# Last attention step: the initial state's reset-gate product and the last probabilities' transposes ahead of the other tile's transposed attention

## The reference, cut to what matters

```python
x = x + attn(cond(x, ...), W_attn, b_attn, W_proj, b_proj)       # 32 heads of 8 features, causal softmax
x = x + ffn(gru(cond_2048, x, W_ih, W_hh, b_ih, b_hh), weight, scale_weight, bias)
return x

# gru, one step; the initial h is cond_2048 (128, 256)
gi = x_t @ W_ih + b_ih          # i_r, i_z, i_n
gh = h @ W_hh + b_hh            # h_r, h_z, h_n
r = sigmoid(i_r + h_r); z = sigmoid(i_z + h_z)
n = tanh(i_n + r * h_n)
h = (1 - z) * n + z * h
```

## Time and profile before

| | us |
|---|---|
| median of 3 runs | 446.46 |
| lowest, highest | 446.11, 447.05 |
| the profiled execution, whole | 447.21 |
| its span, first to last instruction | 445.4 |
| PE busy in the span | 425.4 (95%) |
| DVE, ACT, POOL busy | 329.2, 234.5, 89.9 |

### The profile page before, as it was taken

How to read it: one execution, slowest core, us unless ns; L and a number is a source line. 1 busy time by engine, 2 the same in 40 slices (tenths; PEclk the granted TensorE clock), 3 DMA queues, 4 the chain that set the end, 5 groups by cost and what they waited for, 6 DMA issues and landing times.

```text
span 445.4 us, 13421 instructions
## 1 busy us (share of the span) xinstructions
PE 425.4 (95%) x5448; PEld 351.7 (79%) x5448; DVE 329.2 (74%) x1001; ACT 234.5 (53%) x547; POOL 89.9 (20%) x108
## 2 busy tenths in 40 slices
PE   8799899999999999999999899999999999999994
PEld 6556687786778777787787688899999999999984
DVE  3596888798788887888778945566777767777665
ACT  7254748566575576755766653444444444444341
POOL 7662233333132221322235300000000000000000
PEclk9989999999999999999999999999999999999999
DMA  8941513314132141331212100001010000000001
GB/s 293 396 173 44 154 34 90 90 50 119 31 93 91 49 119 40 91 92 55 74 29 83 38 1 1 1 2 47 1 49 18 30 24 26 24 25 25 24 25 71
DMA packets 34268, 30.36 MB, mean 68 GB/s; under 512 B 4128, under 2 KB 29344, under 8 KB 34208
## 3 DMA queue, kind: packets, MB, share of 16 engines
q1 hardware_dynamic: 34208, 29.51, 20.3%
HBM read 16.92 MB, written 8.39 MB: 57 GB/s over the span
## 4 chain that ended last, share of the span: by engine, by line
PE 75%; DVE 14%; ACT 4%; issue 3%; SPq 2%; DMA 1%; POOL 1%; DVEq 0%; ACTq 0%; POOLq 0%
PE ps_a L1243 9%; PE ps_s L1406 7%; PE ps_t L1406 6%; PE ps_o L1406 6%; PE ps_s L1303 6%; PE ps_s L1462 5%; PE ps_t L1462 5%; PE ps_a L1462 4%; PE ps_m L1462 4%; PE ps_t L1316 4%; PE ps_m L1345 4%; PE ps_o L1327 3%; PE ps_m L1337 2%; ACT y L586 2%; DVE st L889 2%
## 5 line engine op out<-in xcount | busy, mean ns | idle before, releaser
L528 POOL TENSOR_TENSOR sc<-masked,mx 128x512 f32<-128x512 f32 x32 | 45.7, 1429 | 144.1 <-DVE mx L939 144.1
L1243 PE MATMUL ps_a<-yT_r,w_qkv_r 128*128 128x512 f32 x180 | 46.0, 403 | 1.3 <-DVE yT_r L912 0.9
L931 DVE COPY_PREDICATED masked<-kst,ps_s 128x512 f32<-128x512 int32 x64 | 43.9, 734 | 2.9 <-PE ps_s L1303 2.5
L730 ACT ACTIVATE zg<-ps_t,brz 128x128 f32<-128x128 f32 x64 | 20.1, 365 | 39.7 <-PE ps_t L1406 37.4
L939 DVE TENSOR_REDUCE mx<-masked 128x16 f32<-128x512 f32 x64 | 40.5, 674 | 0.0
L624 ACT ACTIVATE sc<-sc 128x512 f32<-128x512 f32 x64 | 37.3, 622 | 5.5 <-DVE sc L945 4.2
L1243 PEld LDWEIGHTS ps_a<-yT_r,w_qkv_r 128*128 128x128 f32 x180 | 32.6, 188 | 9.6 <-issue 2.8
L1077 DVE SCALAR_TENSOR_TENSOR rg<-ps_o,vec,rg 128x128 f32<-128x128 f32 x64 | 19.5, 346 | 24.6 <-PE ps_o L1406 23.6
L557 ACT ACTIVATE pT<-ps_t 128x512 f32<-128x512 f32 x64 | 34.8, 595 | 4.9 <-PE ps_t L1316 3.6
L1406 PEld LDWEIGHTS ps_s<-hT,w_hh 128*128 128x128 f32 x256 | 33.1, 191 | 5.0 <-DVE hT L1095 2.9
L1303 PE MATMUL ps_s<-kbd,qn 64*32 64x256 f32 x1024 | 36.0, 382 | 0.0
(11 more groups left out here) (157 smaller groups left out, 828.1 us busy)
## 6 DMA issues: line engine op xcount, KB each, us to landing
xf<-in_x_feat SPq DMA_DIRECT2D x8, 512.0 KB, 9.5
xg<-in_x_tok SPq DMA_DIRECT2D x8, 512.0 KB, 4.0
kbd<-kn SPq DMA_DIRECT2D x128, 32.0 KB, 1.9
v_dram<-vn SPq DMA_DIRECT2D x16, 256.0 KB, 3.3
vbd<-v_dram SPq DMA_DIRECT2D x64, 64.0 KB, 2.0
out_feat<-ost SPq DMA_DIRECT2D x16, 256.0 KB, 2.0
w_qkv<-in_wqkv SPq DMA_DIRECT2D x1, 768.0 KB, 9.8
w_ih<-in_wih SPq DMA_DIRECT2D x1, 768.0 KB, 13.3
```

What stands on the lines that cost most here:

```text
L528: nc.gpsimd.tensor_tensor(shifted, kept, m.unsqueeze(2).to_broadcast([P, NH // 2, S]), ALU.subtract).then_inc(sc_sub[1], 1)
L730: nc.scalar.activation(dst[:, c, :], gate_part(gate, c, t), ACT.Sigmoid, bias=brz[:, b0 + c:b0 + c + 1]).then_inc(done, 1)
L931: nc.vector.copy_predicated(kept, keep.unsqueeze(1).to_broadcast([P, NH // 2, S]), ps_s[:, h * 512:(h + 1) * 512].rearrange("p (h k) -> p ...
L1243: last = nc.tensor.matmul(bank, w_qkv_r[a][:, c, first_col + m * P:first_col + (m + 1) * P], yT_r[b][:, c, :], start=(a == b == c == 0), s ...
```

## The change

In the last step alone (n = 31), PE's reset-gate product of the initial state moves from behind `probs_v(31)` to the very front of the step, with its two waits, and `transpose_probs(31)` moves in front of `transpose_attn(30)`. On ACT the two copies of `probs_out(31)` move in front of the copy of `attn_out(30)`. DVE, POOL and SP keep their order, and no instruction is added or removed.

```diff
@@ ACT, tile_step @@
+                if n == NT - 1:
+                    probs_out(n)
                 if n > 0:
                     attn_out(n - 1)
-                probs_out(n)
+                if n < NT - 1:
+                    probs_out(n)
@@ PE, tile_step @@
                 if n == 1:
                     pe.wait_ge(kw_out, EARLY)
+                if n == NT - 1:
+                    pe.wait_ge(l_gru, 4 * DMA)
+                    pe.wait_ge(sc_out, 2 * NT)
+                    from_state(0, ("r",), first=True)
+                    transpose_probs(n, n % 2)
                 if n > 0:
                     transpose_attn(n - 1)
                 if norm_ahead and i == 2:
                     pe.wait_ge(q_out, 2 * g + 4)
                     spread_proj(g + 2, ps_a)
-                transpose_probs(n, n % 2, first=(n == 0))
+                if n < NT - 1:
+                    transpose_probs(n, n % 2, first=(n == 0))
...
                 probs_v(n, g, i)
-                if n == NT - 1:
-                    pe.wait_ge(l_gru, 4 * DMA)
-                    pe.wait_ge(sc_out, 2 * NT)
-                    from_state(0, ("r",), first=True)
```

## The result

| | before | changed |
|---|---|---|
| median of 10 runs each, us | 446.50 | 447.65 |
| lowest, highest | 446.11, 447.05 | 446.57, 448.61 |
| ratio, 95% interval | | 1.0022 [1.0013, 1.0030] |
| profiled execution, whole; span | 447.21; 445.4 | 447.97; 446.2 |

In this timing the changed kernel is slower by 0.22%, about 1 us, with the interval from 0.6 to 1.3 us. Two executions of the kernel before, of 1042.68 and 1049.26 us on later occasions, are left out of every ratio. The prediction was 447.1, +0.15%, in a range of 446.1 to 448.0. It gave "within 0.2%" a chance of 0.66 and "slower by more" 0.30; the measured 0.22% lies just beyond the border of the two, and its interval reaches to both sides.

What follows compares the result with a forecast made beforehand. PE, busy 95% of the span, was taken as the bound. The last step's delay, +0.61 at the projection, +0.66 at the reciprocal, +0.67 at `transpose_attn(31)`, gave 446.46 + 0.67 = 447.1 us, range 446.1 to 448.0.

Steps and rivals of the forecast that it cites:

- The product is covered at its old place: Reset-gate product behind `probs_v(31)`: DVE's `on` alone gives 260.04, so taking the product away frees nothing; cost 0 in the hole.
- the rival in the expectation: Expectation for moving the product alone: the product stood on the chain (1.09 us of it), so about -1.0 us; no chance given.
- The new wait: PE waits for tile 30's `oT`, copied after both `pT` copies until 257.88; projection at 257.94 against 257.33, 0.61 later.
- From the projection to `on`: Last step: `probs_v(31)` starts at 258.93, reciprocal of tile 31 at 259.83 (+0.66), `transpose_attn(31)` at 260.70, +0.67 after idle.
- The first load and the reciprocal: Projection's first weight load not hidden (passes 1.16 us); DVE's reciprocal 0.70 after the residual additions start; by the rows +0.67.
- The prediction's other sum: Tile 30's projection: weights in place when the wait for `oT` ends, taking 0.10 off the 1.16, so +0.57.
- Rival A: Last step: filling PE's hole pays off, projection of tile 30 at about 257.17, everything 0.16 earlier, 446.3; chance 0.10.
- Rival B: An unexplained PE "issue" stall of 0.43 us falls into `probs_v(31)`: +1.10, 447.6; chance 0.12.
- Rival C: The recurrent part's first steps have slack towards `xf` and absorb the delay: 446.5; chance 0.07.
- Rival D: PE's clock falls to the lower level at the new holes, about +1 us per eight passes, 448 and more; chance 0.03.

Runs made afterwards that it cites:

- the second trace of the changed kernel: The changed kernel run once more with no edit; distance from last exponential to first product with `xf` 8.06 us, timed ratio 1.0003 [0.9994, 1.0011].
- the order in which it nearly can: Changed kernel, but tile 30's attention transposed and copied between the probabilities' two halves on PE and ACT; distance 7.45 us, ratio 0.9998 [0.9985, 1.0010].

## Why the prediction was right

*The product is covered at its old place.* Right, and shown by moving it alone (7.34 against 7.35). In the trace of before, the product's end and `on` fall on the same moment; the chain of waits named the product, and it would have been wrong to book its 1.09 us as a gain. The gain of 1.0 us that the rival in the expectation forecast did not come.

*The new wait.* Right: the copy to `oT` was put at 257.88, plus the 0.07 by which this execution was later, 257.95; measured 257.96. The projection was put at 257.94, and measured at 258.01. The new holes were put at 0.2, 0.7 and 1.0 and are 0.25, 0.74 and 0.92. For the first, that is luck: counted as the rows count a hole, from the last end to the next start, the prediction's own times leave 0.04 (256.29, 256.33). PE came 0.23 us earlier to it than worked out (254.54 for the product, against 254.70 + 0.07), and in the second trace of the changed kernel, where PE came later, the eight transposes run through without a hole (1.18 us). This hole costs nothing either way, since the second half waits for the exponential. The copy to `oT` right behind a copy to `pT` was the operation that no row of before showed. It started 0.49 after it, and I had taken 0.48 from two `pT` copies.

*From the projection to `on`.* One term was off: `probs_v(31)` starts 1.09 us after the start of a projection that has waited, where I had 0.99 from the projection of tile 31, which has other products behind it. All kernels here in which `probs_v` follows such a projection show 1.09 (256.71 to 257.80, 257.44 to 258.53). It costs 0.05 in the end, because `residual(30)` had been the later by 0.05 and now `probs_v(31)` is: the reciprocal starts 0.05 after its end (259.90, 259.95). The sum was +0.67, and the traces give +0.71.

*The first load and the reciprocal.* The first load was not hidden: in the changed kernel PE's weights and products for the projection both start at 258.01, and its passes take 1.16. The prediction's other sum, with a hidden load, was mis-stated: with a hidden load, `residual(30)` would come 0.10 earlier, but `probs_v(31)` not, and the reciprocal would wait for it until 259.78, so +0.62 and not +0.57; the lower bound of +0.55 had no row behind it. The reciprocal did not wait for the additions to finish: it starts at 259.95, and they end at 259.21 + 0.80 = 260.01. The prediction left out half of what it cites: the Trainium skill, page "VectorE: DVE Perf Modes", section "The DRAIN you can't avoid", adds that a next operation that is not held starts earlier. This start, 0.06 us before the end, agrees with that; whether this reciprocal counts as not held, no run here tests.

*Rival A*, the hole pays off, with `oT` ready before PE: it does not, since ACT can't. Building the order in which it nearly can brought 7.45, still not faster than before. Its price counts one transpose twice: PE would be free at 256.83 + 0.23 = 257.06, not 257.17. *Rival B*, a stall on top: the "issue" hole is the same 0.18 before `probs_v(30)`, and none came behind. (It would have cost less than the +1.10 given: by the prediction's own 0.05, 0.43 - 0.05 = 0.38 reaches the end, +1.05. And in the old order 82 matmuls stand before `probs_v(31)`, not 90, since the product is behind it.) *Rival C*, absorbed: 182.4 us from the first product with `xf` to the end, in both. *Rival D*, a falling clock: not in the changed kernel but once in before, at +1.63. I had given it 0.03, and only against the change.

*The time.* The range of 446.1 to 448.0 holds an unchanged kernel too (446.5), so that the time fell into it proves little; what bears the prediction out is the path through the last step. The traces' +0.71 lies inside the first interval (0.6 to 1.3 us) and not inside the second (-0.3 to 0.5). That the first timing came out higher than the trace, and the second lower, is in keeping with an opening that scatters by more than a microsecond; how much of each comes from that, the timed runs can't tell.

## What to carry to other kernels

Taking an instruction off the chain that ended last gains only as much as the next-latest path ends before it: look for the other producer of the same wait, here DVE's `on` at 259.98 beside PE's 260.04. Work moved into one engine's hole must be followed on the engine that reads it, since an early result that queues behind somebody else's wait (here `probs_v` behind the projection, and its copy ahead of `oT`) costs instead of gaining; the remedy was to move the consumer too. When the opening scatters by more than the effect, measure from an event ahead of the change to one behind it, in several traces.

## What the runs showed that was not expected

The granted clock fell to 0.50 behind a 1.63 us hole in one execution of before and stayed there for about 3.6 us of dense PE work, while it stayed at 1.00 behind holes of 1.42 (twice), 1.22 and 2.66 us. By these five holes the width of the last one alone doesn't decide it; nothing here shows what does. A projection that has waited for its operand delays a following `probs_v` by 1.09 us instead of 0.99, although the state's product behind such a projection starts after 0.99 (260.95, 261.94).
